# Loading the next weight slab behind the cast instead of behind the matmuls

## The reference

```python
h = layernorm(x) * (1 + ca) + sa
f_pre, i_pre, h_pre = h @ W_f.T + b_f, h @ W_i.T + b_i, h @ W_h.T + b_h   # each 1024 -> 1024
diff = softplus(-f_pre) - softplus(-i_pre)
log_f, log_i = -softplus(diff), -softplus(-diff)
# state_t = exp(log_f) * state_(t-1) + exp(log_i) * g(h_pre): a scan over the 2048 positions
x = x + ga * state
x = x + gb * ffn(layernorm(x) * (1 + cb) + sb)    # 8-bit activations, ternary weights, 1024 -> 4096 -> 1024
```

## Time and profile before

| | us |
|---|---|
| median of 3 timed runs | 2611.18 (2610.62 to 2617.02) |
| the profiled execution | 2611.0 |
| span of its slowest core (core 1), first to last instruction | 2609.4 |
| spans of the eight cores | 2591.1 to 2609.4 |
| mixer's matmuls on core 1, first to last | 435.56 to 759.98 |
| matmul busy time in the mixer (768 matmuls) | 189.6 |

### The profile page before, as it was taken

The page is one execution under the profiler, slowest core; times in us unless marked ns, Lnnn a source line. Parts: engine busy times, 40 slices in busy tenths (PEclk is TensorE's granted clock), DMA queues, the critical chain, the costliest instruction groups (busy, mean ns, idle before and its releaser), DMA issues.

```text
span 2609.4 us, 14795 instructions; the slowest of 8 cores (2591.1 to 2609.4 us)
## 1 busy us (share of the span) xinstructions
PE 921.4 (35%) x3428; PEld 339.0 (13%) x3428; DVE 1414.2 (54%) x1180; ACT 529.4 (20%) x452; POOL 190.8 (7%) x180
## 2 busy tenths in 40 slices
PE   0783333554543010047778201101011020163844
PEld 0110011221220000013333000000000000021321
DVE  1000043335534658876666674999999999711011
ACT  0213312413433211112323102121211212000000
POOL 0001000101000000022222110000000000000000
PEclk9895566777776555579989655556565555587977
DMA  6765300110000000012222671112121111376975
GB/s 195 268 233 193 145 1 24 49 44 29 25 25 32 0 1 0 0 57 105 105 105 85 197 217 49 56 65 81 40 81 51 70 71 50 99 247 226 303 248 198
DMA packets 71846, 265.45 MB, mean 102 GB/s; under 512 B 7632, under 2 KB 8016, under 8 KB 64336
## 3 DMA queue, kind: packets, MB, share of 16 engines
q1 hardware_dynamic: 36896, 155.20, 17.6%
q0 software_dynamic: 18304, 67.12, 7.1%
q10 hardware_dynamic: 16560, 42.19, 5.0%
HBM read 214.15 MB, written 50.33 MB: 101 GB/s over the span
## 4 chain that ended last, share of the span: by engine, by line
DVE 49%; DMA 17%; PE 13%; ACT 9%; issue 8%; DVEq 2%; POOL 1%; ACTq 1%; SPq 0%; POOLq 0%
DVE X L100 21%; DVE Hh L100 13%; DVE SC L100 8%; PE PB L734 6%; PE PB L1335 4%; DMA W1Q<-w2qsp 4%; DMA SC<-w2T 4%; ACT X L100 2%; DVE M L100 2%; DMA out_img<-SC 2%; DMA SC<-xT 2%; ACT SC L100 2%; ACT WSB L100 2%; DMA WSTG<-w2T 2%; ACT Hh L100 2%
## 5 line engine op out<-in xcount | busy, mean ns | idle before, releaser
L100 DVE TENSOR_TENSOR SC<-PB,BS 128x512 f32<-128x512 f32 x160 | 110.7, 692 | 299.6 <-PE PB L1335 211.6
L734 PE MATMUL PB<-Hh,WSB 128*128 128x512 bf16 x768 | 189.6, 413 | 189.2 <-POOLq L56 132.2
L100 DVE TENSOR_TENSOR X<-X 128x2048 bf16<-128x2048 bf16 (+1 forms) x120 | 206.8, 1723 | 15.5 <-DVE X L100 2.5
L1052 PE MATMUL PB<-Hh,W1Q 128*128 128x512 bf16 x512 | 126.3, 410 | 227.2 <-POOLq L56 193.7
L1294 PE MATMUL PB<-Hh,M 128*128 128x512 bf16 x128 | 45.0, 529 | 307.3 <-DVEq L56 307.3
L100 DVE TENSOR_SCALAR X<-X 128x2048 bf16<-128x2048 bf16 (+1 forms) x145 | 139.0, 959 | 24.2 <-DVE Hh L100 4.9
L100 ACT ACTIVATE X<-X 128x4096 bf16<-128x4096 bf16 (+1 forms) x24 | 73.2, 3049 | 372.4 <-DVEq L56 371.4
L1294 PE MATMUL PB<-X,RB 128*128 128x512 bf16 x128 | 45.5, 534 | 281.6 <-DVEq L56 281.6
L100 ACT ACTIVATE X<-SC,CPF 128x512 bf16<-128x512 f32 x128 | 92.5, 723 | 216.5 <-DVEq L56 214.3
L1052 PE MATMUL PB<-Hh,RB 128*128 128x512 bf16 x512 | 121.0, 397 | 30.9 <-DVEq L56 30.8
L100 DVE TENSOR_TENSOR Hh<-Hh 128x4096 bf16<-128x4096 bf16 x56 | 128.4, 2292 | 5.8
(11 more groups left out here) (176 smaller groups left out, 1520.5 us busy)
## 6 DMA issues: line engine op xcount, KB each, us to landing
X<-h1qsp SPq DMA_DIRECT2D x96, 512.0 KB, 12.1
SC<-w1T POOLq DMA_DIRECT2D x32, 512.0 KB, 6.0
WSTG<-w1T SPq DMA_DIRECT2D x32, 512.0 KB, 3.4
h1sp<-X POOLq DMA_DIRECT2D x32, 512.0 KB, 3.0
WSTG<-wmodT SPq DMA_DIRECT2D x6, 2048.0 KB, 11.4
SC<-wmodT SPq DMA_DIRECT2D x12, 1024.0 KB, 9.6
SC<-w2T SPq DMA_DIRECT2D x12, 1024.0 KB, 8.1
SC<-w2T ACTq DMA_DIRECT2D x10, 1024.0 KB, 7.5
```

Source lines behind the costliest of these rows:

```text
L100: ins = f(*a, **k)
L734: E.matmul(PB[pp + gi][:, :], WSB[:, gi * 1024 + k * 128: gi * 1024 + (k + 1) * 128], ntile(Hh, k, j), start=(k == 0), stop=(k == KC - 1)),
L1052: E.matmul(PB[jp][:, :], w1q[hc % 4][:, k * 128:(k + 1) * 128], ntile(Hh, k, j), start=(k == 0), stop=(k == KC - 1)),
```

## The change

The first transfer of slab e (e = 1 to 7) waits for the cast of slab e - 1 instead of the matmuls of slab e - 1. The cast of slab e, which overwrites the `WSB` that the matmuls of slab e - 1 read, now waits for these matmuls as well as for its transfers. Slab 0 keeps its waits. No instruction is added or removed, and no buffer either.

```diff
+    cast_pls = {}
...
             if gi == 0 and e >= 1:
-                wv = [("sMM", p.cnt["sMM"])]
+                wv = [("sPL", cast_pls[e - 1])]
...
-        p.on("gpsimd", slab_cast, wait=[("sMW", mw_now)] +
-             ([("sAC", p.cnt["sAC"])] if e == 0 else []), inc=("sPL", 1))
+        cw = [("sMW", mw_now)]
+        cw += [("sMM", p.cnt["sMM"])] if e >= 1 else [("sAC", p.cnt["sAC"])]
+        p.on("gpsimd", slab_cast, wait=cw, inc=("sPL", 1))
+        cast_pls[e] = p.cnt["sPL"]
```

## The result

The change takes the median from 2610.90 us (10 runs, 2606.84 to 2617.02) to 2584.93 us (10 runs, 2575.69 to 2597.17). The ratio is 0.9900, with a 95% interval of 0.9881 to 0.9918: 26.0 us less, where 25.7 were forecast. All of it lies in the mixer. From slab 0's first load to the last mixer matmul the eight cores took 331.9 to 335.2 us before (mean 333.9) and 307.2 to 307.9 after (mean 307.6), 26.3 us less. The spans, averaged over the cores and over all executions, fell by 26.7 us (2600.4 us in the 19 executions of the kernel before that were timed beside the first four experiments, 2573.7 us in 11 with the change).

A forecast was written before the change was run, and what follows sets the result against it. Bound by serial waits in the mixer: load, cast, then matmuls before odd slabs; VectorE's queue in even ones. From 2611.0 us, 24.7 of hidden loads and 1.0 of clock gave 2585.3, stated as 2585.5 us; range 2577 to 2594.

The forecast's parts named there:

- The four loads before odd slabs: Loads of slabs 1, 3, 5, 7 hide under the previous matmuls: 6.17 us saved each, 24.7 us in all.
- the bound on that step: POOL's reaction to the last matmul before an odd slab, at once to 0.5 us: 23.5 to 25.5 us saved.
- The three loads before even slabs: Loads of slabs 2, 4, 6 also hide, but VectorE's chain covers them: worth 0 on the path.
- The casts: Mixer casts move beside the last tile's evacuation without collision; ending the even-slab collision gains 0, at most 0.2 us three times.
- rival B: Mixer casts collide with the last tile's evacuations, up to 7.5 us lost: 2592.8 us, chance 0.13.
- The clock: TensorE's clock nearly always falls in the 4.0 us gaps before odd slabs; shorter gaps gain 1 us in all.
- the prediction's three bounds: Clock in four odd bursts: holds, 8.6 us gained; falls early and returns late, 1.7 lost; short-gap loss from L1052, 1.8 gained.
- the one of rows 7: Each odd burst loses 1.7 us to the clock, as after short gaps in stage L1052; 1.8 us gained overall.
- Rival A: TensorE's clock holds in the 4 us gaps before odd slabs, 8.6 us more gained: 2577.7 us, chance 0.10.
- Rival C: Load before odd slabs was hidden anyway or another wait fills the gap; nothing won: 2611 us, chance 0.03.
- D: Clock stays at 1.2 GHz through each odd burst, 42.4 us long, 76.2 us lost: 2662 us, chance 0.01.

The follow-up runs named there:

- first four experiments: Early load for even slabs only (2613.34 us), odd slabs only (2587.61 us); cast in three steps on the change (2572.78 us), on the kernel before (2600.59 us).
- even-only kernel: The change with the early load kept for slabs 2, 4 and 6 alone; odd slabs wait for the matmuls again: 2613.34 us, ratio 1.0011.
- reordered versions: Two evacuations of slabs 2, 4, 6 put between the scans on VectorE, on the change with two bf16 buffers 2541.76 us, on the change alone 2565.00 us.
- odd-only kernel: The change with the early load kept for slabs 1, 3, 5 and 7 alone; even slabs wait for the matmuls again: 2587.61 us, ratio 0.9915.

## Why the prediction was right

**The four loads before odd slabs.** Forecast 6.17 us each; measured, on core 1 in both kernels, gaps of 10.19, 10.23, 10.17 and 10.16 us that became 4.04, 4.07, 4.04 and 4.04, 24.6 us; averaged over the cores, 24.9. POOL reacts to the last matmul as fast as to its transfer (0.19 us), so the bound on that step was wider than needed.

**The three loads before even slabs.** Forecast 0; the even-only kernel measured 1.0011 (0.9995 to 1.0027). That it is VectorE's queue which covers them is shown by the reordered versions, where the same waits shrink with that queue, and by the stretch from the end of an odd slab to the restart, 43.6 us in every version that keeps VectorE's order and one buffer.

**The casts.** Forecast no collision at the new place and no gain at the old one; both hold, the second also by the odd-only kernel, where the collision is back and the chain as long. The prediction had compared 20.59 us with the collision to 20.42 without and allowed 0.2 us for it. These were the first and the last pair, and the difference is one of the pairs: in the kernel before, pairs two and three collide too and take 20.41 and 20.43 us on core 1, and with the change the first pair takes 20.6 without a collision. So rival B falls by the first 3.38 us cast beside an evacuation.

**The clock.** Forecast 1 us gained, since it would fall nearly always; measured 1.2 us, mean over the cores (92.4 to 91.2 us for the four odd bursts). On core 1, which the prediction worked with, it was 2.2 us: 93.4 us, the longest of the eight cores, became 23.46 + 3 x 22.57 = 91.2. Of the prediction's three bounds the one of rows 7 (1.7 us lost in each burst) was the true one in three of four: 22.57 - 20.88 = 1.69 us. The rate behind them was off: the full-rate burst is 20.9 us and not 21.2, so low clock had cost 9.8 us before on core 1, and not 8.6. The 0.221 us of rows 7 are the length of a short burst divided by its matmuls; the 64 more matmuls of a burst of 96 take 20.88 - 7.07 = 13.81 us, 0.216 each. Rival A, that the clock holds, is refuted: at 4.04 us it fell before every odd slab, on cores 1 and 2 three times at about the restart and once within the gap. Gaps of 1.7 us kept it; between these two lengths no run here has a gap before an odd slab.

**Sum.** On core 1, 24.6 + 2.2 = 26.8 us, and the mixer went from 334.2 to 307.3 us, 26.9. Averaged over the cores, 24.9 + 1.2 = 26.1 of 26.3 us. So the forecast of 25.7 us rests on its mechanism and on sizes that were each nearly right. Rival C is refuted by the gaps, D by the bursts: on core 2 the clock was back 3.8 us after the restart of slab 1 at the latest, in slab 3 some time after 551.0, and the slowest odd burst took 23.54 us, far from 42.

## What to carry to other kernels

When a single staging buffer is refilled only once its second reader is done, look at what the refill really overwrites: here the cast had freed it 24 us earlier or more, and a wait moved to the instruction that needs it gave 1.0% for nothing. Before counting such gaps by their number, follow each to what is late next: four of seven lay on the path, the other three only changed the place of a longer wait. And the longer wait that hides a gain is itself the next thing to look at: taking the evacuations of two tiles ahead of a scan gave nearly as much again as the change (20 us), and with a second bf16 buffer as well the kernel is 2.75% below the kernel before.

## What the runs showed of the hardware

The clock's fall can come after the idle time has ended. With gaps of 4.04 us before odd slabs it was mostly full throughout the gap and half for some 3.5 us of matmuls after it; in odd slabs with 1.7 us of idle time ahead the bursts show no fall, with 7.9 and 10.2 us all do. A gap of 4.04 us therefore costs about 5.7 us (4.04 + 1.69) where the clock falls at the restart, and about 6.7 (4.04 + 23.54 - 20.88) where it falls within the gap; one of 1.7 us just itself.

In the odd-only profile cores 0 and 1 ran bursts of up to 27.3 us, in stretches at a granted clock of 0.81, where the six others had 22.6 to 23.6 us. Core 1, a window of it:

```profile
475.00:480.00 5.00, 5.00 (x21) 2.08 (x20) 1.50 (x2) 1.37 (x2) 0.00 (x0) 0.81 0.00 0
```

The Trainium skill (TensorE: Matmul & The Clock Gate, section "Part 1: The HAM clock gate") describes a limiter that takes a whole die to 13/16 of the clock once three of its cores run dense matmuls. The figure agrees with the 0.81. That it takes the whole die does not: cores 2 and 3 had full clock in the same stage (1.00 in the same window, which each core counts from its own first instruction). Whether this limiter was at work, no run here shows.
